# VectorE work handed to ScalarE and GpSimd, and a new build-time order of the tasks, in a chain of attention blocks

## The reference, cut to what matters

```
x += attn_q(ln1(x));  x += attn_q(ln2(x), ctx);  x += geglu(ln3(x))     # layer 0: quantised attentions A1, A2
x += attn(rms(x));    x += attn(rms(x), ctx);    x += swiglu(rms(x))    # layer 1: SA, CA
x += mha(ln(x), ln(ctx_tok));  x = x + bias;  u = drive(ln(x))          # layer 2: MH, 8 heads
# rms(x) = x * rsqrt(mean(x*x) + 1e-6) * w
# attn_q: _fq(x, delta, zp) = (clip(round(x/delta) + zp, 0, 255) - zp) * delta  on q, k, v and on the softmax
```

## Time and profile before

| | |
|---|---|
| time, median of 3 runs | 3121.27 us (3119.44 to 3128.48) |
| the profiled execution | 3128.91 us, span 3127.2 us |
| busy | PE 2520.2 (81%), DVE 1899.8 (61%), ACT 1297.8 (42%), POOL 1023.1 (33%) |
| mean granted TensorE clock | 0.843 of 2.4 GHz |
| instructions | 47208 |

### The profile page before, as it was taken

How to read it: one execution, slowest core, us unless ns; L and a number is a source line. 1 busy time by engine, 2 the same in 40 slices (tenths; PEclk the granted TensorE clock), 3 DMA queues, 4 the chain that set the end, 5 groups by cost and what they waited for, 6 DMA issues and landing times. The chain is left out here.

```text
span 3127.2 us, 47208 instructions
## 1 busy us (share of the span) xinstructions
PE 2520.2 (81%) x16568; PEld 1811.3 (58%) x16568; DVE 1899.8 (61%) x4639; ACT 1297.8 (42%) x3243; POOL 1023.1 (33%) x903
## 2 busy tenths in 40 slices
PE   4369888898888888898989898888888765448997
PEld 3247676666666766575767666666666442334443
DVE  4975666776766576868686767676764320004766
ACT  1534344545443345454444544344432211224654
POOL 3841132423242233343333334242321010005775
PEclk9679898898888989898989898979888765558999
DMA  4220011101111011111111111110110000001110
GB/s 187 45 52 10 20 18 24 38 21 21 31 31 24 18 28 31 31 25 27 35 24 29 30 24 28 23 28 22 28 25 7 5 18 23 0 0 34 35 37 22
DMA packets 222407, 90.45 MB, mean 29 GB/s; under 512 B 205280, under 2 KB 212784, under 8 KB 221424
## 3 DMA queue, kind: packets, MB, share of 16 engines
q1 hardware_dynamic: 215728, 67.68, 10.9%
q10 hardware_dynamic: 6464, 19.93, 1.7%
HBM read 27.80 MB, written 9.44 MB: 12 GB/s over the span
## 5 line engine op out<-in xcount | busy, mean ns | idle before, releaser
L775 POOL TENSOR_SCALAR work<-work 128x1024 bf16<-128x1024 f32 x128 | 466.6, 3650 | 319.4 <-DVE work L1285 260.6
L1002 PE MATMUL psum<-hT,w_l 128*128 128x256 f32 x2048 | 490.1, 397 | 19.2 <-ACT hT L1356 9.4
L1002 PEld LDWEIGHTS psum<-hT,w_l 128*128 128x128 f32 x2048 | 401.6, 199 | 90.5 <-ACT hT L1356 14.0
L734 POOL TENSOR_TENSOR rstd<-ms,half 128x2 f32<-128x2 f32 (+1 forms) x144 | 101.5, 706 | 850.1 <-DVE ms L1089 446.1
L1456 ACT ACTIVATE work<-psum 128x1024 f32<-128x1024 f32 (+1 forms) x224 | 222.0, 1021 | 284.9 <-PE psum L934 251.8
L1440 ACT ACTIVATE work<-psum,nbias,qs 128x256 f32<-128x256 f32 x512 | 281.6, 565 | 122.4 <-DVE nbias L1194 120.4
L827 PE MATMUL psum<-hT,w_l 128*128 128x256 f32 x896 | 249.4, 433 | 14.7 <-ACT hT L1356 13.5
L836 PE MATMUL psum<-w_l,xhat 128*128 128x256 f32 x640 | 198.2, 464 | 50.1 <-DVE xhat L1265 34.7
L1014 PE MATMUL psum<-w_l,work 128*128 128x256 f32 x1024 | 231.9, 385 | 2.4 <-DVE work L1318 2.1
L827 PEld LDWEIGHTS psum<-hT,w_l 128*128 128x128 f32 x896 | 189.7, 219 | 58.1 <-issue 18.7
L1356 ACT ACTIVATE hT<-psum,cols 128x256 f32<-128x256 f32 x256 | 121.9, 530 | 230.4 <-PE psum L818 229.3
(11 more groups left out here) (183 smaller groups left out, 4719.7 us busy)
## 6 DMA issues: line engine op xcount, KB each, us to landing
w_l<-in_w_l ACTq DMA_DIRECT2D x1, 5120.0 KB, 25.1
x_res<-in_x SPq DMA_DIRECT2D x16, 256.0 KB, 2.8
res<-x_res ACTq DMA_DIRECT2D x16, 256.0 KB, 2.4
w_l<-res SPq DMA_DIRECT2D x16, 256.0 KB, 2.8
out<-w_l ACTq DMA_DIRECT2D x16, 256.0 KB, 2.0
w_l<-in_w_l ACTq DMA_DIRECT2D x1, 3072.0 KB, 13.4
work<-work SPq DMA_TRANSPOSE x192, 3.1
w_l<-in_w_l SPq DMA_DIRECT2D x2, 1024.0 KB, 8.5
```

What stands on the lines that cost most here:

```text
L775: eng.tensor_scalar(rounded_part(a, u, i, p), e_part(a, u, i, p), MAGIC, -MAGIC, ALU.add, ALU.add) \
L1002: mm = eng.matmul(banks.tile(key)[:, h * TOKENS:(h + 1) * TOKENS], w1[:, k, h, m * P:(m + 1) * P], hT[p][:, k, :], start=(k == 0), stop=(k ...
```

## The change

Work leaves VectorE in four places. (1) The scaling of q, k, v of A1 and A2 out of PSUM moves to ScalarE (`scale_up`: `Identity` with scale 1/delta and bias MAGIC, which rounds); VectorE then clips in one operation (`bounded`). (2) The RMS norms: ScalarE squares with a running sum (`squares_of`), VectorE only adds the epsilon, and ScalarE also scales (`normalise`). (3) The second operation of A2's `round` moves to GpSimd as `whole`, and A2's subtraction on VectorE waits for the `whole` of two parts earlier before it writes the same buffer. (4) `nbias` and `rsum` change from `tensor_scalar` to `scalar_tensor_tensor` with a tile of ones as second input; the arithmetic is the same.

On GpSimd A1's `round` becomes two operations, times one plus MAGIC in place, then minus MAGIC times one into bf16; only the second waits for the earlier transpose to have read its target.

The plan gets new durations, a `lag` behind a task (a DMA's landing, now without holding its queue), 1.3 us (`SWITCH`) ahead of a ScalarE task that needs another function table than the last one, and takes as equal all tasks that could start within 0.2 us (`NEAR`) of the first. The core of the diff:

```diff
-TURN, LAND = 2.5, 2.5
-HOP = 0.15
+LAND = 2.0
+HOP, NEAR, SWITCH = 0.15, 0.2, 1.3
...
+def table_of(task):
+
+    engine, kind, what = task[0:3]
+    if engine != "scalar" or kind not in ("exps", "hidden"):
+        return None
+    return what if kind == "hidden" else "exp"
...
-                    starts[t] = start, spans
+                    starts[t] = start + (SWITCH if table_of(t) not in (None, table) else 0.0), spans
             first = min(start for start, _ in starts.values())
-            t = min((t for t in starts if starts[t][0] <= first), key=lambda t: (t[4], at[t]))
+            t = min((t for t in starts if starts[t][0] <= first + NEAR), key=lambda t: (t[4], at[t]))
             start, spans = starts[t]
             ready.remove(t)
+            table = table_of(t) or table
             for (key, _, reader), span in zip(self.fills[t], spans):
...
-        q = work.add("vector", "moments", name, 0, p, 1.0, *before)
+        rms = NORMS[name][1] is None
+        if rms:
+            before = [work.add("scalar", "squares", name, 0, p, 1.45, *before)]
+        q = work.add("vector", "moments", name, 0, p, 0.25 if rms else 1.45, *before)
         q = work.add("pool", "rstd", name, 0, p, 0.7, q)
         used = earlier(p, "tensor", "norm", "lnu", 0) if name == "ln1" else None
-        x = work.add("vector", "normalise", name, 0, p, 0.75, q, used)
+        x = work.add("scalar" if rms else "vector", "normalise", name, 0, p, 0.95, q, used)
         used = earlier(p, "scalar", "store", None, 0) if name == "ln1" else None
...
-                        fills=[((what[0], a.name, p), 1, (reader, what, a, 0, p))])
+                        fills=[((what[0], a.name, p), 1, ("scalar" if a.quant else reader, what, a, 0, p))])
+        if a.quant:
+            full = work.add("scalar", what, a, 0, p, 0.75, full, *before)
+            return work.add("vector", what, a, 0, p, us, full)
...
                 e = work.add("scalar", "exps", a, (u, i), p, 3.1 if a.self_attn else 0.75, e)
-                e = work.add("vector", "probs", a, (u, i), p, 2.1 if a.self_attn else 1.4, e)
+                e = work.add("vector", "probs", a, (u, i), p, 2.0 if a.self_attn else 1.25, e)
                 if not a.self_attn:
                     e = work.add("pool", "probs", a, (u, i), p, 1.25, e)
-                e = work.add("pool" if a.self_attn else "vector", "round", a, (u, i), p, 2.05 if a.self_attn else 1.0, e,
+                e = work.add("pool" if a.self_attn else "vector", "round", a, (u, i), p, 2.25 if a.self_attn else 0.55, e,
                              turned.get(2 * u + i - HELD))
+                if not a.self_attn:
+                    e = work.add("pool", "whole", a, (u, i), p, 0.8, e, turned.get(2 * u + i - HELD))
                 rounds[2 * u + i] = e
-                turned[2 * u + i] = work.add("sync", "turn", a, (u, i), p, TURN, e,
-                                             weighed if a.self_attn else None, v if a.self_attn else None)
+                turned[2 * u + i] = work.add("sync", "turn", a, (u, i), p, 1.25, e,
+                                             weighed if a.self_attn else None, v if a.self_attn else None, lag=LAND)
                 evacuated.append(turned[2 * u + i])
...
                 def round_off(a, part, p):
                     u, i = part
+                    eng.wait_ge(*norm_step.at(("up", a.name, u, i, p)))
+                    e = e_part(a, u, i, p)
+                    eng.tensor_scalar(e, e, 1.0, MAGIC, ALU.mult, ALU.add).then_inc(*even.next((a.name, u, i, p)))
+                    eng.wait_ge(*even.at((a.name, u, i, p)))
                     if 2 * u + i >= HELD:
                         eng.wait_ge(*turned[part_slot(u, i, p)].at((a.name, *before(u, i), p)))
+                    eng.tensor_scalar(rounded_part(a, u, i, p), e, -MAGIC, 1.0, ALU.add, ALU.mult) \
+                        .then_inc(*probs_ready_p.next((a.name, u, i, p)))
+
+                def whole(a, part, p):
+                    u, i = part
                     eng.wait_ge(*norm_step.at(("up", a.name, u, i, p)))
-                    eng.tensor_scalar(rounded_part(a, u, i, p), e_part(a, u, i, p), MAGIC, -MAGIC, ALU.add, ALU.add) \
-                        .then_inc(*probs_ready_p.next((a.name, u, i, p)))
-
-                steps = {"rstd": rstds, "bias": bias, "zeros": zeros, "spread": spread, "probs": probs, "round": round_off}
+                    if 2 * u + i >= HELD:
+                        eng.wait_ge(*turned[part_slot(u, i, p)].at((a.name, *before(u, i), p)))
+                    eng.tensor_scalar(rounded_part(a, u, i, p).rearrange("p (c n) -> p c n", n=P)[:, :, 0:CTX],
+                                      e_part(a, u, i, p).rearrange("p (c n) -> p c n", n=CTX), -MAGIC, 1.0, ALU.add, ALU.mult) \
...
+                    elif NORMS[name][1] is None:
+                        eng.wait_ge(*squares.at((name, p)))
+                        eng.tensor_scalar(ms[q][:, :], mv[q][:, :, 0], NORMS[name][2], None, ALU.add).then_inc(*moments.next(("ms", name, p)))
...
-                    inv = qs[0:rows, ATTENTIONS.index(a), "qkv".index(what):"qkv".index(what) + 1]
-                    eng.wait_ge(*banks.at(key))
-                    eng.tensor_scalar(tmp, bank, inv, 127.0, ALU.mult, ALU.min) \
-                        .then_inc(*banks.released(key, quant, (1, key)))
-
-                def rounded(tmp, key, signal, result):
-                    eng.wait_ge(*quant.at((1, key)))
-                    eng.tensor_scalar(tmp, tmp, -128.0, MAGIC, ALU.max, ALU.add).then_inc(*signal.next(result))
+                def bounded(tmp, key, signal, result):
+                    eng.wait_ge(*scaled.at(key))
+                    eng.tensor_scalar(tmp, tmp, MAGIC + 127, MAGIC - 128, ALU.min, ALU.max).then_inc(*signal.next(result))
...
                     if a is A1:
-                        eng.tensor_scalar(nbias[:, r, 0:4], m, qs[:, ATTENTIONS.index(a), 4:5],
-                                          None, ALU.mult).then_inc(*max_ready.next(("max", a.name, u, i, p)))
+                        eng.scalar_tensor_tensor(out=nbias[:, r, 0:4], in0=m, scalar=qs[:, ATTENTIONS.index(a), 4:5],
+                                                 in1=onesp[:, 0:4], op0=ALU.mult, op1=ALU.mult).then_inc(*max_ready.next(("max", a.name, u, i, p)))
                         return
+                    if 2 * u + i >= HELD:
+                        eng.wait_ge(*whole_ready.at((a.name, *before(u, i), p)))
                     eng.tensor_tensor(e_part(a, u, i, p).rearrange("p (r c n) -> p r c n", r=2, c=4), s,
                                       bcast(m.unsqueeze(3), [P, 2, 4, CTX]), ALU.add) \
                         .then_inc(*banks.released(key, max_ready, ("max", a.name, u, i, p)))
...
+                    eng.scalar_tensor_tensor(out=rsum[:, r, mine], in0=rden[:, r, mine], scalar=qs[:, ATTENTIONS.index(a), 3:4],
+                                             in1=onesp[:, mine], op0=ALU.mult, op1=ALU.mult) \
                         .then_inc(*norm_step.next(("p", *key)))
...
                     eng.wait_ge(*probs_ready_p.at((a.name, u, i, p)))
...
-                        eng.wait_ge(*turned[part_slot(u, i, p)].at((a.name, *before(u, i), p)))
-                    eng.wait_ge(*norm_step.at(("up", a.name, u, i, p)))
-                    eng.tensor_scalar(rounded_part(a, u, i, p).rearrange("p (c n) -> p c n", n=P)[:, :, 0:CTX],
-                                      e.rearrange("p (c n) -> p c n", n=CTX), -MAGIC, None, ALU.add) \
-                        .then_inc(*probs_ready_v.next((a.name, u, i, p)))
 
...
 
+                def squares_of(name, n, p):
+
+                    q = p % STREAMS
+                    eng.wait_ge(*res_ready.at((BEFORE[name], p)))
+                    for m in range(TT):
+                        ins = eng.activation(xhat[p][:, m, :], x_res[p][:, m, :], ACT.Square, scale=D ** -0.5, accum_out=mv[q][:, m, 0:1])
+                    ins.then_inc(*squares.next((name, p)))
+
+                def normalise(name, n, p):
+                    eng.wait_ge(*rstd_ready.at((name, p)))
+                    for m in range(TT):
+                        ins = eng.activation(xhat[p][:, m, :], x_res[p][:, m, :], ACT.Identity, scale=rstd[p % STREAMS][:, m:m + 1])
+                    ins.then_inc(*xhat_ready_a.next((name, p)))
+
+                def scale_up(a, what, tmp, bank, p, rows=P):
+
+                    key, n = (what, a.name, p), "qkv".index(what)
+                    eng.wait_ge(*banks.at(key))
+                    eng.activation(tmp, bank, ACT.Identity, bias=magic[0:rows, :], scale=qs[0:rows, ATTENTIONS.index(a), n:n + 1]) \
+                        .then_inc(*banks.released(key, scaled, key))
+
```

More of the change, by code:

```diff
@@ L72, with add @@
 BEFORE = {"ln2": "a1", "ln3": "a2", "sa_n": "geglu", "ca_n": "sa", "mlp_n": "ca", "lnq": "swiglu", "lnu": "mh"}
+def table_of(task):
[3 more added lines that the diff above has]
+    return what if kind == "hidden" else "exp"
```

(26 more changed lines are left out.)

101 lines of the change are left out of this document (49 added, 52 removed).

## The result

The changed kernel takes 3171.80 us (median of 4 runs, 3167.61 to 3173.84), the kernel before beside it 3124.65 (4 runs, 3119.44 to 3128.48): ratio 1.0142, 95% interval 1.0121 to 1.0163. It is slower by 1.4%; forecast was 3031, in a range of 2920 to 3155.

A forecast was written before the change was run, and what follows sets the result against it. Bound taken as a mixture: a short VectorE-led stretch and a long one nearly filling TensorE. 2.3 + 2.0 - 1.0 + 2.1 = 5.4 us per period, times 15.2 is 82, plus 8 at the start: 3031 us, range 2920 to 3155.

The forecast's parts named there:

- The plan: Planner's new durations, table-change price and tie rule: new order's effect taken as 0, bounds -5 and +9 us per period.
- The prediction's own sign of being wrong: VectorE's busy time falls as said but the period does not, or the period moves by more than 10 us.
- VectorE's two terms and ScalarE's: Per period: VectorE's relief gains 2.3 us at 1302 to 1343 us and 2.0 elsewhere; ScalarE's 12 queue entries cost 1.0.
- the dense stretch: 1302 to 1343 us, two streams in attention, VectorE full: half of 4.7 us relief, 2.3 per period, was counted.
- The rounding: A1's rounding on GpSimd, 2.1 instead of 3.65 us, eight a batch: 2.1 us gained per period, bounds 6.2 and -1.4.
- The start: From 100 to 200 us, VectorE busy 84 of 100: its relief there was to save 8 us.
- ScalarE in VectorE's place: Rival: norm and projection entries queue behind A1's exponentials on ScalarE, -6.8 us per period, 3216 us; chance 0.13.
- VectorE behind GpSimd: Rival: A2's subtraction waits for GpSimd twice a batch, at worst 8.0 us, -2.6 per period, 3153 us; chance 0.09.
- Slow multiply-add: Rival: the rounding's multiply-add on GpSimd is as slow as add-add, gain 1.9 us per period, 3084 us; chance 0.08.
- The low-clock stretch closed: Rival: the new order closes the 23.9 us at 1.2 GHz, 9 us more per period, 2894 us; chance 0.13.
- The rule on the shared port: VectorE instructions with two SBUF inputs contend with GpSimd reading SBUF: `nbias` and `rsum` edit taken as 0, bounds 0 and 1.8.

The follow-up runs named there:

- the first experiment: The changed kernel's new operations, with every engine's list and PSUM bank as the kernel before had them: 3096.66 us, ratio 0.9921.
- i1: The kernel before, all its operations unchanged, put task for task into h1's list: 3015.03 us, ratio 0.9661.
- h1: The kernel before with only the two-step rounding new, in its planner grid's shortest list (streams 40 us apart, hop 0.2, ties 0, table change 1.3): 3000.77 us.
- g2: The kernel before with no new operations, in the changed kernel's list made with ties 0.3 us and table change 2.0: 3189.16 us, ratio 1.0207.
- g1: As g2, same list, but with the rounding in two steps as the only new operation: 3210.11 us, ratio 1.0281.
- h2: The kernel before with no new operations, in its planner grid's shortest list (streams 30 us apart, hop 0.1, ties 0.2, table change 0): 3234.63 us.
- i2: All the new operations put into h1's list, moved tasks standing where VectorE's tasks stood: 2992.68 us, ratio 0.9583.
- h3: Complete changed kernel, planner set to streams 40 us apart, hop 0.2, ties 0.6, table change 3.0, the decoder's list kept old: 3253.63 us.

## Why the prediction was wrong

**The step that failed** is in *The plan*: "What the new order itself does to the meeting of streams I cannot derive from the rows: I take 0." It does -75/15.2 = -4.9 us per period (the first experiment against the changed kernel), the lower end of the bounds of -5 and +9 given there. Of the 141 us between forecast and measurement the order makes 75; the other 66 are the operations, which gave 24.5 where 90 were forecast. With the order's 75 the forecast would have been 3106: the order explains the wrong direction, and the operations' terms are the second failure. The upper side was no fancy either: the good order gives the operations of before 103 us (3118.33 to 3015.03), 6.8 per period, and not by closing the low-clock stretch. A term with the widest bounds of all had to carry the range and the chances; the range ended at 3155 because the slower cases were all made of waits for an operation, and a worse list was no rival of its own. The prediction's own sign of being wrong came: VectorE's busy time fell as said, and the period did not. Why this list is worse than the old one is told only in what it does, longer waits and more time at the lower clock; which meeting of the streams makes them is open.

**VectorE's two terms and ScalarE's**, 2.3 + 2.0 - 1.0, or 50 us over 15.2 periods: measured 1 in the old order, 8 in the good one, neither firmly told from zero. VectorE's busy time fell as said, by (1899.8 - 1732.5)/16 = 10.5 us a batch against about 12, and ScalarE's rose by (1404.5 - 1297.8)/16 = 6.7, less than 12, with 26 fewer table loads. The time that VectorE gained was covered; even the half that I took in the dense stretch was not there, since all that leaves VectorE adds 1 us to the rounding's 24. And i1 shows that the period did not need that relief to get shorter: it keeps all of VectorE's work, and the period falls by 6.

**The rounding**, 2.1 a period or 32 us: right in kind, 24 in the old order and some 14 in the good one. Its two halves cost 1.065 and 1.058 where I had 2.1 together.

**The start**, 8 us: the first `drive` comes at 367.0 instead of 368.9, so 2.

**The rivals.** ScalarE in VectorE's place: fell with the first experiment, though its sign (waits for L1373 above 37 us) was there; a sign that two mechanisms share decides nothing. VectorE behind GpSimd: L1204 with 2.2 us of idle time. Slow multiply-add: 1065 ns. The low-clock stretch closed: the time at the lower level grew, the mean clock fell from 0.843 to 0.825.

**The rule on the shared port** (the Trainium skill, SBUF — State Buffer, section Who interferes with whom) was rightly weighed: L1285 with its second SBUF input averages 453 ns where L1278 had 443, so the edit is worth nothing there, as I took it; `nbias`, whose mean rose from 277 to 347 ns, got no faster either.

**Still open:** which meeting of the streams makes the changed kernel's list slow, which of the planner's numbers makes h1's list good (streams 40 us apart, hop, ties, table change were moved together), whether the scalings cost something on ScalarE, and why g2 with the longer rounding is faster than g1. The changed kernel's own list was not run with the operations of before.

## What to carry to other kernels

In a kernel whose lists are made by a planner, an edit of durations or of tie rules is an edit of every engine's order, and for the operations of before that was worth anything from 112 us lost (h2) to 103 won (i1), while all the new operations, in one and the same list, were worth 22 to 25. Measure the two apart: new operations in the old order, old operations in the new one, and give each set of operations a list of its own before you credit either. Among six lists for the same operations the planner's own length ranked the times, so it is the first thing to look at, but it depends on what the planner counts, and it did not foresee h2. This kernel had 3.4% waiting there without a single instruction changed.

## What the runs showed of the hardware that was not expected

On GpSimd, the same 128x1024 rounding takes 3650 ns as add and add in one instruction and 1065 + 1058 = 2123 ns as multiply-add and add-multiply in two, one of them writing float32. On ScalarE a 128x256 square with a running sum takes 409 + 190 ns, less than the exponential of the same size, which reads PSUM (566 + 207 in the changed kernel); a 128x512 `Identity` out of PSUM with both bias and scale from tiles takes 778. With all the new operations TensorE's 16568 matmuls are busy from 2459.9 us (i2) to 2560.1 (h3), by the order alone: the order counts twice, in idle time and in the busy time of the matmuls. Between the first experiment and the changed kernel the mean granted clock falls with it (0.847 to 0.825, 48.4 us more busy time); between the kernel before and i1 it is 0.843 in both, and 37.0 us of busy time go all the same, so the mean clock is not the whole of it.
